# A head's score row in the lone stage: broadcast from DRAM into SBUF in place of TensorE into PSUM, with eleven of sixteen blocks compared on ScalarE

## The reference

```
# layer 0: 16 heads of 32 features, additive scores
h      = relu(layernorm(x))
seq    = (h @ W_seq).reshape(N, 16, 32)
s1, s2 = seq . a1, seq . a2                       # one number per head and node
scores = leaky_relu(s1[:, :, None] + s2[:, None, :], 0.2) + (1 - adj) * -65500
x      = x + elu(softmax(scores) @ seq @ W_out + b_out)
# layer 1: one head, dot-product scores, entries that are 0 after the mask become -10000
h = relu(layernorm(x));  q, k, v = h @ W_q.T + b_q, h @ W_k.T + b_k, h @ W_v.T + b_v
z = (q @ k.T) / sqrt(512) * adj;  z = where(z == 0, -10000, z)
out = x + relu(softmax(z, axis=1) @ v)
```

## Time and profile before

| | us |
|---|---|
| median of three runs | 498.7 |
| the profiled execution's own time | 501.12 |
| its span, from the first to the last instruction | 499.6 |
| the lone stage in it, from its first wait to the last evacuation's start | 113.25 to 214.96 |

### The profile page before, as it was taken

How to read it: one execution, slowest core, us unless ns; L and a number is a source line. 1 busy time by engine, 2 the same in 40 slices (tenths; PEclk the granted TensorE clock), 3 DMA queues, 4 the chain that set the end, 5 groups by cost and what they waited for, 6 DMA issues and landing times.

```text
span 499.6 us, 6189 instructions
## 1 busy us (share of the span) xinstructions
PE 396.3 (79%) x2033; PEld 287.0 (57%) x2044; DVE 371.2 (74%) x715; ACT 244.4 (49%) x511; POOL 273.6 (55%) x283
## 2 busy tenths in 40 slices
PE   2899999994979888886778698889890499896950
PEld 2788888783867777852546454555680255443520
DVE  2999999977899898958679898778511478987300
ACT  1579777848888697823222344353510342342310
POOL 1344422236886776866705877774567268861330
PEclk9699999997999898999797988999997599997995
DMA  7979997300002432354413344531246347863450
GB/s 268 409 292 363 362 354 288 127 31 3 8 7 27 125 88 87 91 167 150 133 61 103 111 128 147 171 131 62 106 152 209 102 105 150 168 143 46 62 64 3
DMA packets 24290, 70.00 MB, mean 140 GB/s; under 512 B 6208, under 2 KB 6464, under 8 KB 22080
## 3 DMA queue, kind: packets, MB, share of 16 engines
q0 software_dynamic: 14336, 42.63, 31.0%
q1 hardware_dynamic: 9536, 26.96, 14.7%
q10 hardware_dynamic: 384, 0.00, 0.0%
HBM read 52.45 MB, written 17.12 MB: 139 GB/s over the span
## 4 chain that ended last, share of the span: by engine, by line
DVE 28%; PE 17%; POOL 15%; issue 10%; DMA 4%; ACT 1%; SPq 0%; DVEq 0%; ACTq 0%
PE psum L1331 6%; POOL record_dram L1127 4%; PE psum L1278 3%; PE psum L1234 3%; POOL s_shared L1147 3%; POOL s_shared L1165 3%; POOL s_rs L1176 2%; DVE s_shared L835 2%; DVE w_seq L929 2%; DVE s_shared L769 2%; DMA s_shared<-seq_dram,tab 2%; DVE s_shared L762 2%; DVE s_shared L760 2%; DVE s_st L853 2%; DVE s_x L851 2%
## 5 line engine op out<-in xcount | busy, mean ns | idle before, releaser
L1008 ACT ACTIVATE s_shared<-psum,seq_all 128x320 bf16<-128x320 f32 x192 | 81.6, 584 | 15.2 <-PE psum L1234 11.1
L1234 PE MATMUL psum<-s_shared 128*128 128x198 bf16 x768 | 76.4, 261 | 8.6 <-POOL s_shared L1147 8.6
L1234 PEld LDWEIGHTS psum<-s_shared 128*128 128x128 bf16 x768 | 71.5, 101 | 14.6 <-POOL s_shared L1147 10.3
L532 PE MATMUL psum<-w_seq,hT 128*128 128x272 f32 x256 | 63.2, 402 | 0.0
L1256 PE MATMUL psum<-w_out,hT 128*128 128x512 f32 x128 | 60.7, 620 | 0.9 <-ACT hT L1042 0.5
L1278 PE MATMUL psum<-w_qk,s_early 128*128 128x257 f32 x240 | 57.4, 393 | 0.0
L532 PEld LDWEIGHTS psum<-w_seq,hT 128*128 128x128 f32 x256 | 48.9, 195 | 10.0 <-issue 0.3
L1278 PEld LDWEIGHTS psum<-w_qk,s_early 128*128 128x128 f32 x240 | 46.5, 199 | 7.0
L1054 ACT ACTIVATE h_t<-s_x,s_nm,s_rs 128x512 f32<-128x512 f32 x16 | 13.0, 814 | 64.6 <-DVE s_nm L864 64.6
L1165 POOL DMA_INDIRECT s_shared<-seq_dram,tab x28 | 34.9, 1246 | 10.8 <-issue 8.2
L456 DVE MAX8 near<-adj_ring 128x8 f32<-128x2048 f32 x16 | 36.5, 2284 | 5.7 <-DMA adj_ring<-in_adj_dram 5.7
(11 more groups left out here) (249 smaller groups left out, 783.3 us busy)
## 6 DMA issues: line engine op xcount, KB each, us to landing
adj_ring<-in_adj_dram SPq DMA_DIRECT2D x16, 1024.0 KB, 7.5
seq_dram<-seq_all POOLq DMA_DIRECT2D x16, 264.0 KB, 3.7
x_ring<-in_x_dram SPq DMA_DIRECT2D x16, 256.0 KB, 8.2
w_seq<-in_L_gnn_W_seq_dram SPq DMA_DIRECT2D x1, 1024.0 KB, 6.1
w_q<-in_L_gnn_W_q_dram SPq DMA_DIRECT2D x1, 1024.0 KB, 14.7
w_k<-in_L_gnn_W_k_dram SPq DMA_DIRECT2D x1, 1024.0 KB, 16.6
w_v<-in_L_gnn_W_v_dram SPq DMA_DIRECT2D x1, 1024.0 KB, 8.2
w_out<-in_L_gnn_W_out_dram SPq DMA_DIRECT2D x1, 1024.0 KB, 10.9
```

What stands on the lines that cost most here:

```text
L532: last = pe.matmul(bank[2 + 2 * (t % 2) + i][:, 0:SX // 2], hT[:, t % 2, c * P:(c + 1) * P], w_seq[:, c, i * (SX // 2):(i + 1) * (SX // 2) ...
L1008: last = act.activation(ind[i][:, j, PAD:], bank[4 + i][:, 0:LN], ACT.Sign, bias=seq_all[:, j, D + n:D + n + 1])
L1234: last = pe.matmul(acc(i)[:, k, 0:3 * W2], ind[i][:, j, k * P:(k + 1) * P], rhs.rearrange("p t w -> p (t w)"), start=(j == 0 and k != 1), ...
```

## The change

Heads 0 and 1 keep their PE broadcast into PSUM. For the others the row comes by DMA:

- PE makes one more matmul at the stage's start, which sums the three bf16 parts of s1 for all 16 heads (16 x 320) in bank 2. ACT copies it to SBUF, SP stores it to a new DRAM tensor and waits, and then loads rows 2 to 10, each repeated over 128 partitions, into six row buffers in the place of `w_seq`, which is free by then. A buffer is loaded again when `sign_done` and `twos_done` say that both readers of its last row have finished. Rows 11 to 15 come behind the three table loads on SP.
- ACT and DVE read that row from SBUF instead of PSUM, for heads 2 to 15.
- SIGNS goes from 12 to 11: ACT compares 11 blocks in every head, DVE 5.
- PE no longer broadcasts between the heads' products.

```
-SIGNS = 12
+SIGNS = 11
+ROWS = 6
...
+        s1_dram = nc.dram_tensor("s1_dram", [H, LN], F32, kind="Internal").ap()
...
+        s1_f = hT[0:H, 1, 0:LN]
+        s1_rows = w_seq[:, :, :].rearrange("p c n -> p (c n)")[:, 0:ROWS * LN].rearrange("p (r n) -> p r n", r=ROWS)
...
+        def row_of(eng, n, b):
+            if n < 2:
+                eng.wait_ge(bc_done, n + 1)
+                return bank[b + n][:, 0:LN]
+            eng.wait_ge(row_loaded[n % ROWS], 16 * ((n - 2) // ROWS + 1))
+            return s1_rows[:, n % ROWS, :]
...
                 def twos(n):
                     i = n % 2
-                    dve.wait_ge(bc_done, n + 1)
+                    s1 = row_of(dve, n, 6)
                     for j in range(SIGNS, T):
-                        last = dve.tensor_scalar(ind[i][:, j, PAD:], bank[6 + i][:, 0:LN],
+                        last = dve.tensor_scalar(ind[i][:, j, PAD:], s1,
                                                  neg_s2[:, j - SIGNS, n:n + 1], 2.0, ALU.is_gt, ALU.mult)
...
             def _(act):
+                act.wait_ge(s1_summed, 1)
+                act.activation(s1_f, bank[2][0:H, 0:LN], ACT.Copy).then_inc(s1_ready, 1)
                 for n in range(H):
                     i = n % 2
-                    act.wait_ge(bc_done, n + 1)
+                    s1 = row_of(act, n, 4)
                     if n >= 2:
                         act.wait_ge(mm_done, n - 1)
                     for j in range(SIGNS):
-                        last = act.activation(ind[i][:, j, PAD:], bank[4 + i][:, 0:LN],
+                        last = act.activation(ind[i][:, j, PAD:], s1,
                                               ACT.Sign, bias=seq_all[:, j, D + n:D + n + 1])
...
             def _(sp):
+                sp.wait_ge(s1_ready, 1)
+                sp.dma_start(s1_dram[:, :], s1_f).then_inc(s1_stored, 16)
+                sp.wait_ge(s1_stored, 16)
+
+                def load_rows(lo, hi):
+                    for n in range(lo, hi):
+                        if n >= 2 + ROWS:
+                            sp.wait_ge(sign_done, n - ROWS + 1)
+                            sp.wait_ge(twos_done, n - ROWS + 1)
+                        sp.dma_start(s1_rows[:, n % ROWS, :], s1_dram[n, :].partition_broadcast(P)).then_inc(row_loaded[n % ROWS], 16)
+
+                load_rows(2, 11)
                 sp.wait_ge(rec_stored, T * 16)
...
+                load_rows(11, H)
...
+                pe.matmul(bank[2][0:H, 0:LN], pick[:, :], s1t).then_inc(s1_summed, 1)
                 broadcast(0)
                 broadcast(1)
...
                     pe.wait_ge(sign_done, n + 1)
                     pe.wait_ge(twos_done, n + 1)
-                    if n + 2 < H:
-                        broadcast(n + 2)
                     pe.wait_ge(r2_done, n + 1)
```

More of the change, by code:

```diff
@@ L617, in sparse_layers @@
     (x, out, psum, bank, ident, ones, seq_all, w_out, w_qk, wv_t, bias_rows, ones_b, bout_bc, bv_bc, u_bias_bc, h_t, hT, power, w_seq,
-     tab, s2_max, bd, neg_s2, slot_no, seq_dram, h1_dram, record_dram, rank, pick, s1t,
+     tab, s2_max, bd, neg_s2, slot_no, s1_dram, seq_dram, h1_dram, record_dram, rank, pick, s1t,
      rec_stored, tab_loaded, seq_stored) = (v[k] for k in (
          "x out psum bank ident ones seq_all w_out w_qk wv_t bias_rows ones_b bout_bc bv_bc u_bias_bc h_t hT power w_seq "
-         "tab s2_max bd neg_s2 slot_no seq_dram h1_dram record_dram rank pick s1t "
+         "tab s2_max bd neg_s2 slot_no s1_dram seq_dram h1_dram record_dram rank pick s1t "
          "rec_stored tab_loaded seq_stored").split())
@@ L656, in sparse_layers @@
             sem(k) for k in "bc_done sign_done twos_done pad_set r1_done r2_done mm_done evac_done".split())
+        s1_summed, s1_ready, s1_stored = (sem(k) for k in "s1_summed s1_ready s1_stored".split())
+        row_loaded = [sem(f"row_loaded{i}") for i in range(ROWS)]
+        s1_f = hT[0:H, 1, 0:LN]
+        s1_rows = w_seq[:, :, :].rearrange("p c n -> p (c n)")[:, 0:ROWS * LN].rearrange("p (r n) -> p r n", r=ROWS)
         lone_ctx = ctx.enter_context(ExitStack())
```

## The result

The changed kernel takes 511.52 us in the median of four runs (510.5 to 512.6); the kernel before 497.03, with a fourth run (495.06) beside the three above. The ratio is 1.0282 with a 95% interval of 1.0208 to 1.0357: 14.5 us slower, in a forecast of 512 us with a range of 503.5 to 517. The profiled execution took 512.1, its span is 510.5.

A forecast was written before the change was run, and what follows sets the result against it. POOL bounds heads with scatters, DVE later ones; with DVE waiting for POOL, fourteen heads of 6.8 us and 1.43 for tables give +13.0 us, 514.1 against the profiled 501.12; 512 as median, range 503.5 to 517.

The forecast's parts named there:

- DVE's comparison from SBUF waits for POOL.: DVE's comparisons beside POOL's long operation: one held up as the COPY was, 1.95 us a head.
- POOL gets in between.: Start of a head's five DVE comparisons: POOL's long operation goes after the first, before the second.
- A head of 6.8.: Heads without scatters: DVE's chain with the wait for POOL sums to 6.75, taken as 6.8 us, against 5.17.
- the hand-over: Passing between DVE's comparisons and POOL's long operation in each head: some 0.05 us beside 1.95 of waiting.
- POOL's 6.71 stays the limit in heads with three scatters.: Heads with three scatters: POOL bounds them at 6.71 us, DVE's 6.8 beside it; the first scatter's wait shifts to another.
- POOL's operation of head 1 up to 1 us earlier.: L1147 of head 1, at 124.32: up to 1 us earlier, since L760 no longer starts together with the first scatter.
- The sum.: From head 1 to head 15's products: fourteen heads of 6.8 plus 1.43 for tables; +13.0 us in all.
- ACT at 0.46 from SBUF, nothing gained.: ACT's comparisons: 0.46 us from SBUF against 0.43 from PSUM; eleven take 5.06, twelve took 5.15, hidden inside 6.8.
- PE and the clock (rival 3): PE idles 2.3 us a head, so its clock falls too: 514 to 518 us, chance 0.07.
- Row loads in time (rival 4): Rival: rows from DRAM come late and ACT and DVE wait; 3 us more than forecast, chance 0.02.
- Rival 1: DVE finishes all five comparisons before POOL's long operation; a head 6.15 us, kernel 504 to 506, chance 0.18.
- Rival 2: SBUF comparisons and POOL don't hinder each other; a head 5.1 us, gain 1 to 4, 495 to 498, chance 0.17.

The follow-up runs named there:

- DVE's part alone: Kernel before with only DVE's row from SBUF for heads 2 to 15, 4 blocks on DVE, ACT's row from PSUM: 505.15 us, ratio 1.0179.
- all without it: Changed kernel with DVE's row broadcast into PSUM again, five blocks on DVE, ACT's row still from SBUF: 498.47 us, ratio 1.0032.
- the same tile read in another form: Changed kernel, DVE's comparisons from head 2 on as SCALAR_TENSOR_TENSOR, row from SBUF, factor 2.0 from PSUM: 499.78 us, ratio 1.0037.
- the first profile of before: Kernel before, unchanged, in the profiled execution on which the prediction was built: 501.12 us.
- with five blocks: Kernel before with SIGNS = 11 alone, DVE comparing 5 blocks, all from PSUM: 498.62 us, ratio 1.0031.
- the two profiles of before: Kernel before, unchanged, profiled twice: 501.12 us, then 495.88 us.
- The try to turn this into a gain: Kernel before with 11 blocks on ACT in heads 0 to 5, 12 after, all from PSUM: 497.21 us, ratio 0.9969.

## Why the prediction was right, step by step

- *DVE's comparison from SBUF waits for POOL.* Right, and it is the cause. The form alone shows it both ways: DVE's part alone 1.0179, all without it 1.0032, the same tile read in another form 1.0037. The step from a COPY that waited to a TENSOR_SCALAR that would wait as well held. The Trainium skill ("SBUF — State Buffer", section "Who interferes with whom") names both operations among those that can take the pair of ports that DVE shares with GpSimd; this case shows it at 2.07 us for the one that waits. The recorded starts don't tell which of two goes first: in the earlier trace rows the COPY's start (162.61) lies before POOL's (162.72), and still the COPY waited. The evacuation in front of it ended only at 162.69.
- *POOL gets in between.* Right: the second comparison is held, not POOL behind five. POOL's operation is only 0.06 us longer (2.01 against 1.95).
- *A head of 6.8.* It is 6.69, 6.68 in most. I gave 0.05 to the hand-over and rounded 6.75 up; 14 heads make 1.7 us. The first of them took 7.03, behind a PE that needed 10.9 us for heads 0 and 1.
- *POOL's 6.71 stays the limit in heads with three scatters.* Wrong in cause, harmless in size. The first scatter's wait on L760 did not move to another in full: a scatter takes 1092 ns, not 1372, and POOL idles 0.54 us for DVE behind each three scatters (2.28 behind two). DVE bounds them, at 6.71 by accident.
- *POOL's operation of head 1 up to 1 us earlier.* Right, and a little more: 123.22 against 124.32.
- *The sum.* Head 15's products were forecast 13.0 later than in the first profile of before, at 223.5, and found at 222.08: +11.6, and the whole execution +11.0 (512.1 against 501.12). That is 2 us too much in the sum. The medians say +14.5, since the profile of before stood 4.1 us above its median and not 2.4, and the profile of the changed kernel 0.6 above its own; of three runs one could not know it. The two errors have opposite signs. That the mechanism and the 6.7 us of a head came out is no luck; that the median lies within 0.5 us of the forecast is in part.
- *ACT at 0.46 from SBUF, nothing gained.* Right: 11 in 5.09 us, 0.463, and idle 24.7 us for PE in the stage.
- *PE and the clock (rival 3).* The clock came down in three heads beyond the first two, each with 6.0 on PE at a mean granted clock of 0.72, between its two levels, 1.2 and 2.4 GHz. PE had idled 2.83, 3.73 and 2.22 us before them, but 2.26 also before a head (147.06) that kept 1.00. All three slow heads were hidden in the 6.7 of a head. It needed no extra price.
- *Row loads in time (rival 4).* Right: no wait on them is in the table of waits.
- *Rival 1* was made real by POOL's added wait: 6.25 a head, forecast 6.15. *Rival 2* was made nearly real by cutting POOL's operation: a gain of 5.5 us, forecast 1 to 4. It is not quite the same case, since the cut also shortens POOL's work in the heads with scatters.

## What to carry to other kernels

Moving this comparison's operand from PSUM to SBUF made it shorter (0.30 us for 0.48) and also made it exclude POOL. Before such a move, look in the timeline for what POOL does in those microseconds: here PSUM comparisons were the cover under which 1.95 us of POOL's work cost nothing, and 0.4 us saved on DVE in a head were paid with 1.95. A short operation with a long maximum, ended with another engine's end, is the sign to look for in the profile of before.

## What I had not expected

- A slower form can be faster: SCALAR_TENSOR_TENSOR with one PSUM source takes 0.48 instead of 0.30 and takes 2.4% off the kernel, since POOL runs beside it.
- Half a microsecond more on DVE in heads bound by POOL's scatters did not lengthen them: from head 1 to head 7 POOL's starts lie 36.8 us apart with five blocks, and 38.4 and 36.8 in the two profiles of before. The try to turn this into a gain showed none (0.9969, 0.9932 to 1.0005).
- Two executions of one kernel differ by 3.85 us in this stage, by how POOL's scatters and DVE's L760 meet, how long POOL waits for the record table and in which heads the clock is low.
